# Attention and a routed feed-forward on one Trainium2 core: the order of the steps on every engine is written anew

## The reference

```python
x = x + layernorm(attention(layernorm(x)))
x = x + layernorm(ffn(layernorm(x)))
# attention: 16 heads of 8, rotary positions, causal
att = softmax(where(causal, q @ k.T / sqrt(8), -1e10));  y = att @ v @ Wp + bp
# ffn: 16 experts of width 176, the best 2 per token by softmax gate, and a shared part of width 352
y = sum over the 2 experts of weight * ((silu(x @ w1 + b1) * (x @ w3 + b3)) @ w2 + b2)
z = (silu(x @ sw1 + sb1) * (x @ sw3 + sb3)) @ sw2 + sb2;  result = y + z
```

## Time and profile before

| | before |
|---|---|
| median of 3 runs | 1276.95 us (1274.19 to 1278.73) |
| profiled execution, its own time | 1279.9 us |
| span of that execution | 1277.7 us |
| mean granted TensorE clock | 0.934 |
| TensorE busy | 1099.5 us, 86% |
| VectorE busy | 867.2 us, 68% |
| ScalarE busy | 703.4 us, 55% |
| GpSimd busy | 840.7 us, 66% |

### The profile page before, as it was taken

How to read it: one execution, slowest core, us unless ns; L and a number is a source line. 1 busy time by engine, 2 the same in 40 slices (tenths; PEclk the granted TensorE clock), 3 DMA queues, 4 the chain that set the end, 5 groups by cost and what they waited for, 6 DMA issues and landing times.

```text
span 1277.7 us, 26879 instructions
## 1 busy us (share of the span) xinstructions
PE 1099.5 (86%) x8520; PEld 711.3 (56%) x8520; DVE 867.2 (68%) x2283; ACT 703.4 (55%) x1569; POOL 840.7 (66%) x984
## 2 busy tenths in 40 slices
PE   1479989999999999999999999999866999999900
PEld 1344555655656565565656656566334788888700
DVE  4386778777787776777778777777222666666676
ACT  0115666565656656565665666666621555555534
POOL 4544558677777767777777776665664466666667
PEclk9768999999999999999999999999887999999955
DMA  4322223313143231323323133223312354454366
GB/s 88 120 80 88 80 62 118 99 54 103 56 122 98 77 101 54 101 69 124 96 65 103 55 104 108 71 75 81 107 44 81 89 157 124 120 156 123 97 212 187
DMA packets 104681, 126.16 MB, mean 99 GB/s; under 512 B 17422, under 2 KB 85344, under 8 KB 99936
## 3 DMA queue, kind: packets, MB, share of 16 engines
q1 hardware_dynamic: 91638, 104.54, 27.9%
q0 software_dynamic: 8704, 18.11, 4.0%
q10 hardware_dynamic: 4202, 1.81, 0.5%
HBM read 78.06 MB, written 45.42 MB: 97 GB/s over the span
## 4 chain that ended last, share of the span: by engine, by line
PE 72%; DVE 15%; issue 3%; DMA 2%; POOL 2%; ACT 1%; SPq 1%; POOLq 0%; DVEq 0%; ACTq 0%
PE heads_ps L1474 11%; PE wide L1502 10%; PE score L1464 10%; PE wide L1624 7%; PE wide L1439 4%; DVE mx L1276 4%; PE wide L1504 4%; PE score L1452 3%; PE wide L1605 3%; PE wide L1606 3%; PE score L1596 2%; PE wide L1535 2%; DVE chosen L1123 2%; PE wide L1622 2%; PE misc L1482 2%
## 5 line engine op out<-in xcount | busy, mean ns | idle before, releaser
L946 ACT ACTIVATE values<-score 128x512 f32<-128x512 f32 (+1 forms) x704 | 370.0, 556 | 199.9 <-PE score L1464 194.1
L1276 DVE TENSOR_REDUCE mx<-wide 128x2 f32<-128x1024 f32 (+3 forms) x384 | 387.6, 1040 | 85.5 <-PE wide L1504 84.8
L833 POOL TENSOR_SCALAR_AFFINE_SELECT values<-values 128x512 f32<-128x512 f32 x256 | 163.8, 643 | 169.0 <-ACT values L946 166.8
L1502 PE MATMUL wide<-qk 72*128 72x512 bf16 (+3 forms) x1024 | 248.8, 310 | 14.1 <-DVE mx L1276 6.0
L1464 PE MATMUL score<-qk 75*128 75x512 bf16 (+3 forms) x1024 | 237.3, 305 | 10.1 <-DMA qk<-mparts 6.2
L878 POOL DMA_INDIRECT token_scratch<-spread,e_id x144 | 137.9, 958 | 96.4 <-issue 74.5
L1504 PE MATMUL wide<-maskneg,identb 128*128 128x128 bf16 x1024 | 201.1, 225 | 0.0
L1474 PE MATMUL heads_ps<-values 128*32 128x512 f32 (+3 forms) x2048 | 176.1, 444 | 0.2 <-issue 0.2
L822 POOL DMA_INDIRECT sorted_scratch<-zr,places x128 | 129.9, 1015 | 56.4 <-DVE places L1217 19.1
L1464 PEld LDWEIGHTS score<-qk 75*128 75x128 bf16 x1024 | 88.0, 99 | 123.2 <-ACT values L946 51.7
L1502 PEld LDWEIGHTS wide<-qk 72*128 72x128 bf16 x1024 | 102.2, 100 | 90.8 <-DVE mx L1276 26.1
(11 more groups left out here) (196 smaller groups left out, 2003.2 us busy)
## 6 DMA issues: line engine op xcount, KB each, us to landing
qk<-parts_scratch SPq DMA_DIRECT2D x192, 192.0 KB
parts_scratch<-spread SPq DMA_DIRECT2D x16, 768.0 KB, 8.3
qk<-sorted_scratch SPq DMA_DIRECT2D x144, 66.0 KB
front<-token_scratch SPq DMA_DIRECT2D x16, 512.0 KB, 3.8
xt<-attn_x SPq DMA_DIRECT2D x16, 256.0 KB, 8.5
xr<-attn_x SPq DMA_DIRECT2D x16, 256.0 KB, 8.9
x_scratch<-z SPq DMA_DIRECT2D x16, 256.0 KB, 6.7
shared_scratch<-s_out SPq DMA_DIRECT2D x16, 256.0 KB
```

The source lines that it names most:

```text
L833: nc.gpsimd.affine_select(out=prob[n][:, :, 0:P], in_=prob[n][:, :, 0:P], compare_op=ALU.is_ge, fill=0.0, base=0, pattern=[[0, HG], [1, P] ...
L946: nc.scalar.activation(free_ap(prob[kb][:, hs_[0], :], [[1, N * len(hs_)]]), score[SCORE_RING.buffer(b, step)][:, 0:N * len(hs_)], ACT.Exp ...
L1276: nc.vector.tensor_reduce(mx[:, h0:h0 + len(hs_), j:j + 1], src, axis=AX.X, op=ALU.max).then_inc(p1_max, 1)
L1502: nc.tensor.matmul(o, q4[e][0:ROWS, h, j * P:(j + 1) * P], k4[e][0:ROWS, h, 0:L], start=True, stop=False)
```

## The change

The three strings are replaced. Every step that was there is still there, with the same instructions. Each engine's order, the order of the users of the ring buffers, and the offsets of some steps differ: among others `chosen`, G0, U0, H0, H1, d0, d1 and d2 go from offset -2 to -1 and stand late in the list; Q and `cos` stand with offset 3 instead of 4; R has offset 4, `zrstd`, Z and `residual` 0; `heads2` of a batch stands in the iteration after it; masks of groups 0 to 2 stand in the iteration before their batch. UPS, the table by which G finds the buffer of its U, is sorted by number, since U0 now stands behind U1 and U2 in the string.

```diff
--- before.py
+++ after.py
@@ -87,27 +87,27 @@
 
 
 ORDER = (
-    "s0.0 p19@0 s0.1 R p20@0 s0.2 v3.1@-1 v3.2@-1 v3.3@-1 s0.3 p21@0 s0.4 heads3@-1 p22@0 mask0.1 s0.5 s0.6 p23@0 "
-    "chosen@-2 H0 mask0.2 v0.0 s0.7 s0.8 d0 G0 Y U0 p0 s0.9 s0.10 K p1 place mask0.3 s1.0 W s1.1 d1 p2 mask1.0 "
-    "s1.2 p3 s1.3 zrstd zstats v0.1 p4 s1.4 s1.5 U1 s1.6 s1.7 V v0.2 M1@0 Z v0.3 mask1.1 N1@0 s1.8 G1 O1@0 stats residual "
-    "s1.9 p5 p6 heads0 s1.10 v1.0 v1.1 s2.0 rstd mask1.2 d2 mask1.3 p7 s2.1 mask2.0 s2.2 normal p8 rrstd rnormal "
-    "s2.3 p9 s2.4 mask2.1 s2.5 rstats T v1.2 mask2.2 v1.3 s2.6 p10 mask2.3 s2.7 second H1 v2.0 s2.8 third0 "
-    "mask3.0 p11 s2.9 heads1 p12 U2 s2.10 G2 p13 s3.0 rX s3.1 H2 d3 mask3.1 d4 v2.1 v2.2 mask3.2 s3.2 third1 "
-    "mask3.3 sin0@4 X@4 sin1@4 s3.3 rL s3.4 d5 v2.3 M0 choose N0 p14 Q@4 O0 s3.5 s3.6 v3.0 mask0.0@1 p15 s3.7 p16 s3.8 "
-    "rexp D s3.9 cos@4 sin2@4 p17 d6 p18 sin3@4 s3.10 heads2 d7 "
+    "s0.0 heads2@-1 s0.1 p18@0 rrstd Q rnormal s0.2 p19@0 mask2.1 s0.3 v3.1@-1 v3.2@-1 v3.3@-1 s0.4 p20@0 s0.5 "
+    "heads3@-1 s0.6 mask2.2 mask2.3 p21@0 s0.7 p22@0 s0.8 K H2 rstd normal mask3.0 s0.9 p23@0 place s0.10 cos Y "
+    "d3 s1.0 v0.0 M1@0 s1.1 N1@0 p0 W mask3.1 s1.2 O1@0 s1.3 v0.1 v0.2 v0.3 zstats d4 mask3.2 p1 s1.4 U1 G1 s1.5 "
+    "mask3.3 p2 v1.0 third0 d5 s1.6 p3 s1.7 p4 s1.8 s1.9 p5 d6 heads0 third1 s1.10 p6 s2.0 p7 s2.1 v1.1 mask0.0@1 "
+    "sin0@4 s2.2 p8 d7 mask0.1@1 s2.3 v1.2 v1.3 H0@-1 p9 s2.4 s2.5 rstats p10 s2.6 U2 G2 s2.7 heads1 sin1@4 s2.8 "
+    "p11 p12 s2.9 stats mask0.2@1 s2.10 T d0@-1 v2.0 M0 s3.0 s3.1 mask0.3@1 V N0 d1@-1 d2@-1 v2.1 mask1.0@1 s3.2 "
+    "rX O0 p13 s3.3 s3.4 zrstd@0 p14 v2.2 sin2@4 v2.3 Z@0 mask1.1@1 s3.5 p15 s3.6 second rL choose sin3@4 s3.7 "
+    "mask1.2@1 mask1.3@1 residual@0 p16 rexp R@4 s3.8 mask2.0@1 H1@-1 X@4 chosen v3.0 s3.9 G0@-1 U0@-1 s3.10 D "
+    "p17 "
 )
 START = (
-    "stats@1 rstd@1 X@1 normal@1 sin0@1 sin1@1 Q@1 sin2@1 cos@1 splits@1 fold@1 sin3@1 R@1 rstd@2 normal@2 "
-    "third0@1 third1@1 stats@2 sin0@2 sin1@2 sin2@2 T@1 sin3@2 R@2 rstd@3 normal@3 third0@2 second@1 X@2 V Q@2 "
-    "cos@2 third1@2 stats@3 sin0 T@2 X sin1 sin2 Q sin3 p0 R rstd p1 normal p2 p3 p4 cos p5 p6 second@2 p7 p8 p9 "
-    "p10 p11 stats p12 T sin0@4 sin1@4 p13 p14 X@4 M0 p15 N0 second O0 Q@4 p16 sin2@4 p17 cos@4 third0 third1 sin3@4 "
-    "mask0.0@1 p18 "
+    "rstd@1 stats@1 normal@1 sin0@1 X@1 sin1@1 sin2@1 sin3@1 R@1 Q@1 rstd@2 normal@2 V stats@2 third0@1 third1@1 "
+    "cos@1 splits@1 fold@1 T@1 second@1 sin0@2 sin1@2 X@2 Q@2 cos@2 stats@3 sin2@2 T@2 X sin3@2 R@2 rstd@3 "
+    "normal@3 third0@2 sin0 third1@2 Q sin1 p0 second@2 p1 p2 sin2 p3 p4 p5 rstd p6 p7 p8 sin3 stats normal p9 R "
+    "p10 p11 third0 p12 p13 mask0.0@1 M0 p14 third1 sin0@4 sin1@4 mask0.1@1 mask0.2@1 X@4 N0 cos sin2@4 mask0.3@1 "
+    "mask1.0@1 mask1.1@1 p15 mask1.2@1 O0 mask1.3@1 p16 sin3@4 p17 T R@4 second mask2.0@1 "
 )
 DRAIN = (
-    "v3.1@-1 v3.2@-1 v3.3@-1 chosen@-2 heads3@-1 K place Y d0 d1 W d2 zstats U0 G0 zrstd Z d3 U1 residual G1 H0 "
-    "rstats U2 rrstd rnormal rX rL G2 choose rexp H1 d4 d5 H2 d6 d7 chosen K@-1 counts@-1 place@-1 blocks@-1 "
-    "ends@-1 D d0@-1 d1@-1 d2@-1 d3@-1 d4@-1 d5@-1 d6@-1 d7@-1 U0@-1 rows@-1 U1@-1 U2@-1 G0@-1 G1@-1 H0@-1 G2@-1 "
-    "H1@-1 H2@-1 D@-1 "
+    "heads2@-1 rrstd rnormal v3.1@-1 v3.2@-1 v3.3@-1 heads3@-1 K H2 place Y d3 W zstats d4 U1 G1 d5 d6 d7 H0@-1 "
+    "rstats U2 G2 d0@-1 d1@-1 d2@-1 rX rL choose rexp H1@-1 chosen G0@-1 U0@-1 D K@-1 counts@-1 H2@-1 place@-1 "
+    "blocks@-1 ends@-1 rows@-1 d3@-1 d4@-1 U1@-1 G1@-1 d5@-1 d6@-1 d7@-1 U2@-1 G2@-1 D@-1 "
 )
 OFFSET = dict(stats=4, rstd=4, normal=4, X=3, Q=3, cos=3, sin=3, R=3, T=3, second=3, third=3, V=1, p=1, M=1, N=1, O=1, s=0, v=0,
               mask=0, heads=0, Y=-1, W=-1, zstats=-1, zrstd=-1, Z=-1, residual=-1, rstats=-1, rrstd=-1, rnormal=-1,
@@ -164,7 +164,7 @@
 
 
 GATE = next(s for s in STEPS if s.what == "rL")
-UPS = [s for s in STEPS if s.what == "U"]
+UPS = sorted((s for s in STEPS if s.what == "U"), key=lambda s: s.n)
 
 
 def program(nc, x, Wq, bq, Wk, bk, Wv, bv, Wp, bp, gate_w, gate_b, w1, b1, w3, b3, w2, b2,
```

## The result

| | before | after |
|---|---|---|
| median | 1277.28 us (1274.19 to 1278.73, 4 runs) | 1213.91 us (1213.65 to 1214.54, 4 runs) |
| ratio, 95% interval | | 0.9508 (0.949 to 0.9526) |
| span of the profiled execution | 1277.7 us | 1211.3 us |
| mean granted TensorE clock | 0.934 | 0.941 |

The forecast was 1239 us, with a range of 1220 to 1266. The change gained 66.4 us of span where 38.1 were forecast.

The account below looks back on a forecast made before the run. TensorE was taken to bound the iterations, so only idle time could be won: 21 + 0.6 + 2 - 1 + 7 + 5 + 3.5 = 38.1 us off 1279.9, forecast median 1239 us, range 1220 to 1266.

Parts of the forecast that it names:

- What bounds the kernel: Full iterations: TensorE bounds them, its 51.7 us busy stay, and a new order can give back only 2.4 of 54.1 us.
- K's wait: TensorE's idle time ahead of step K, waiting for VectorE's `chosen`, goes: 1.8 us gained per iteration.
- New waits: Full iterations: TensorE newly waits for VectorE's run from `zstats` to T or for masks, 0.3 us per iteration, ends 0 and 1.5.
- VectorE becomes the bound: Rival, iterations: T or a `p` comes 1.5 us late in each and the clock keeps dropping, 1259 us; chance 0.20.
- Iterations 3 to 11: Full iterations: each gains 2.4 - 0.3 = 2.1 us besides the clock, 21 us for iterations 3 to 12.
- The best case of the rivals: Rival, whole kernel: no new wait, no clock drop, fill and drain at their better ends, 1222 us; chance 0.07.
- The clock: TensorE's six half-clock stretches go with its waits of near 2 us: 7 us gained, ends 0 and 8.6.
- iteration 15: It gets U0 of batch 14 (1.9 us) and p18, in part into idle time: 1 us longer.
- Iterations 0 and 1: Waits of s2.0 for the maxima's DMA go, 4.3 us, against p18 and U0 moved in: net 2 us gained.
- The fill: Before iteration 0: Q of batch 3 and p18 leave, X and Q of batch 1 come earlier: 5 us gained, ends 2 and 8.
- The drain: After iteration 15: W(15) and SyncE's row blocks start earlier, against U0, D and late scatters: 3.5 us gained, ends 0 and 6.
- The slower case: Rival, iterations: GpSimd passes VectorE's lateness on through late masks, TensorE waits and its clock drops, 1292 us; chance 0.07.

Follow-up runs that it names:

- a_reduce_plus1: The changed kernel with one more VectorE reduction of p10 per iteration, 1.2 us, into a spare tile: 1232.35 us, ratio 0.9656 to the kernel before.
- a_v_split: The changed kernel with its blocks of 32-column `v` products split, six more per iteration: 1290.16 us on a slower chip, ratio 0.9728 to the kernel before.
- a_control: The changed kernel run again, unaltered, for comparison within its set: 1215.14 us, ratio 0.952 to the kernel before.
- a_v_merged: The changed kernel with the lone v1.1 and v2.1 put beside their neighbours, four passages less: 1218.81 us, ratio 0.9551 to the kernel before.
- b_chosen_early: The kernel before with `chosen` moved from behind p23 to behind p20: 1335.46 us on a slower chip, ratio 1.0078 to the kernel before.
- a_chosen_late: The changed kernel with `chosen` put back in front of p21, at offset -2: 1332.46 us on a slower chip, ratio 1.005 to the kernel before.
- a_reduce_plus2: The changed kernel with two more VectorE reductions of p10 per iteration, 2.4 us together: 1312.58 us on a slower chip, ratio 0.9993 to the kernel before.
- a_reduce_plus3: The changed kernel with three more VectorE reductions of p10 per iteration, 3.6 us together, into a spare tile: 1297.7 us, ratio 1.0164 to the kernel before.
- a_scatters_first: The changed kernel with the last batch's scatters d3 to d7 ahead of H1 and H2 in the drain: 1262.17 us, slower chip, ratio 0.9512 to the kernel before.
- a_maxima_mid: The changed kernel with M1, N1 and O1 started at s1.5, not behind v0.0: 1261.47 us on a slower chip, ratio 0.9583 to the kernel before.
- a_scatters_again: The changed kernel with scatters d3 to d7 ahead of H1 and H2 in the drain, a repeat: 1252.15 us, slower chip, ratio 0.9521 to the kernel before.

## Why the prediction missed, step by step

**What bounds the kernel: right as to the engine, wrong as to the floor.** "No step is added or dropped, so the 51.7 us of TensorE's work stay" is the step that failed, and with it "a new order can give back only its idle time: 2.4 us of 54.1". The 51.7 was busy time, and I took busy time for work. A matmul's end is modelled in the profile, so busy time also covers short gaps between the starts. The distances between the starts of steps, in an undisturbed iteration of either kernel (us, before and after):

```
s0.10 (K's wait behind it)  2.17  0.28      K itself    0.59  0.40
s1.9 (p5's wait)            0.75  0.22      s1.0 to W   0.57  0.31
s2.3                        0.41  0.31      p8          0.54  0.45
whole iteration            54.10 50.59
```

K was counted at 1.8 and gave 2.1 (1.90 + 0.19); p5 at 0.4 and gave 0.53; W at 0.2 and gave 0.26. These make 2.9, s2.3 and p8 0.2 more, and the last 0.45 is the sum of some thirty steps of ±0.02 to 0.14, mostly passages to and from `v` and M. a_reduce_plus1 shows the undercount by itself (0.59 shown, 1.0 paid), a_v_split the passages (1.3 us of them, unseen). The Trainium skill ("Perfetto Trace Analysis", "Identifying the Most-Contended Engine") warns that matmul busy share is no good measure of how near TensorE is to its limit, since pipelined instructions look smaller; the trace agrees that the share misleads: from 224 to 740 us a_control is busy for 516.0 us of 516.0 with iterations of 50.6 us, and a_v_merged for 514.3 with 50.9, without one wait in the list.

**New waits, 0.3 us per iteration.** The list shows none, and the distances between steps find under 0.1 us at any one place of the changed kernel: 0.3 x 10 was too much. But the reason I gave, 1.8 to 2.8 us left to VectorE in its run from `zstats` to T, was wrong: the run ends well only as a whole, and inside it each `p` has a deadline of its own, two buffers on. At p11 the margin is about 0.4 us (a_reduce_plus1), at p8 0.5 (a_v_merged). At three places there is none: in the changed kernel itself Y, U2 and p16 start 0.06 us behind the VectorE reduction that frees their buffer (medians of iterations 3 to 11), for instance p16:

```profile
366.67 0.96 DVE L1276 TENSOR_REDUCE mx<-wide 128x2 f32<-128x768 f32 x1 [0.24 <-PE wide L1504]
...
367.68 0.28 PE L1502 MATMUL wide<-qk 72*128 72x256 bf16 x1
```

The rival "VectorE becomes the bound" was wrong by its price (1259 us), but VectorE already touches TensorE at these places, for some 0.03 to 0.08 us each.

**Iterations 3 to 11.** 39.3 us: 7.9 of clock and 31.4 of the rest, 3.5 each, against 2.1. Of the 28.3 us by which the forecast missed the span, 12.5 lie here and 14.8 in iterations 0, 1 and 15; the rest nearly cancels. The best case of the rivals, 1222 us, was 8 us too long as well, for it kept the same floor.

**The clock.** Forecast 7, found 7.9 in iterations 3 to 11, and more in iterations 0, 12 and 15. For the full iterations the reasoning held: each half-clock stretch there followed a wait of TensorE of 1.7 to 2.9 us, in the kernel before, b_chosen_early, a_chosen_late, a_reduce_plus2 and a_reduce_plus3, and none followed one of 0.6 us. But two sentences of it were wrong. The clock was not full up to 252.9 us: it was half from 96 to 103 and from 120 to 123.5, in iteration 0. And the rows that spoke against a clock that small idle times make fall end at 911.6, just short of a stretch that stands behind small idle times alone. The rule of the Trainium skill ("TensorE: Matmul & The Clock Gate", "A second HAM failure mode: psum-queue depth-cycling") is that small gaps between groups of matmuls can make the clock swing. In iterations 2 to 14 of the changed kernel the trace shows nothing of it, with the clock at 1.00; in iteration 15 the kernel before, a_scatters_first and a_v_split agree with it.

**Iterations 0 and 1: forecast 2 us gained, found 9.6; iteration 15: forecast 1 us longer, found 6.2 shorter.** I costed the waits and not the half clock beside them, though the rows of before had it: clock 0.89 in iteration 0 and 0.93 in iteration 15. Kernel before, waits of TensorE from 92 to 140 us, then its clock at two places, and the waits ahead of the second:

```profile
PE wide L1502 <- DVE mx L1276: 2.5, 3, 1.5
PE score L1464 <- DMA qk<-mparts: 2.0, 1, 2.0
...
96.00:103.00 7.00, 6.95 (x36) 3.40 (x35) 4.08 (x5) 2.59 (x6) 4.01 (x5) 0.51 0.71 221
...
912.00:919.00 7.00, 6.98 (x22) 2.86 (x22) 0.55 (x2) 2.81 (x6) 4.30 (x6) 0.52 0.97 301
...
905.23 0.63 PE L1482 MATMUL misc<-ident,oT 128*128 128x128 f32 x4 [0.86 <-DVE mparts L1284]
...
908.19 0.60 PE L1464 MATMUL score<-qk 75*128 75x512 bf16 x2 [0.47 <-DMA qk<-mparts]
909.26 0.88 PE L1464 MATMUL score<-qk 75*128 75x512 bf16 x2 [0.47 <-ACT values L946]
910.35 0.34 PE L1464 MATMUL score<-qk 75*128 75x384 bf16 x1 [0.20 <-ACT values L946]
```

Seven microseconds at half clock are worth up to 3.5 us, and that twice, and 3.4 us more of it stood in iteration 0. For iteration 0 an estimate from the rows adds up: 3.8 us of waits gone (4.9 before, 1.1 after), some 4 us of clock, less 0.55 for p18, against 7.5 found. But no run put one of these back alone. For iteration 15 the clock is shown to be worth such a sum: one wait of 1.5 us put back brings half clock and costs 5.3 us (a_maxima_mid). That is not the wait of the kernel before, though, whose longest was 0.86 us. Which of its four small waits, or all together, brought the half clock there, no run shows.

**The fill: right**, 5 forecast, 4.8 found. Its parts weren't tested.

**The drain: forecast 3.5, found 0.2.** K(15) moved from 32.5 to 32.8 us behind the drain's start, with U0 and D in front of it, and the scatters behind H1 and H2 ended late; I had named both and priced them too low. a_scatters_again gives the price of the second, 2.1 to 2.5 us; the rest of the 3.3 missed is open.

**The slower case** fell outright: no wait of TensorE from 224 to 730 us is left, for a mask or anything else.

## What to carry to other kernels

When the bounding engine is TensorE, take its floor from the distances between the starts of steps where nothing waits, not from its busy time: each wait costs some 0.2 to 0.4 us more than its idle time, each passage between tile shapes about 0.1, and one wait of 1.5 us or more can cost as much again, or more, in half clock. Price a margin at each buffer's own deadline, against whichever engine frees that buffer, not over a whole run of work. And read a granted clock under 1.00 in any stretch, the short ones at the ends too, as time that may be won back with the waits before it, several small ones included.

## What the hardware showed that I had not expected

- The half clock can follow waits shorter than the stretch that it then lasts: 1.72 us idle, then a mean of 0.74 over 6 us; 1.5 us, then 0.71 over 15 us. A wait of that length doesn't always bring it (6 of 10 in the kernel before). The levels are 2.4 GHz (1.00) and 1.2 GHz (0.50).
- It can also come behind small waits alone: 0.86, 0.47, 0.47 and 0.20 us ahead of the stretch at 912 us in the kernel before, 0.45 and 0.20 us in a_scatters_first.
- A passage between 128-column score tiles and 32-column `v` products costs 0.09 to 0.14 us each way and is shown as busy; one between bf16 and f32 over the same 128 columns costs nothing that these distances show (0.17 us for the score step either way).
- A `p` that has to wait starts 0.06 us behind the end of the read that frees its buffer, and a wait so short that the tail of the last matmul covers it is in no list.
- VectorE's L1123, two operands in SBUF, took 2.37 us beside GpSimd's R and 0.29 us away from it. The Trainium skill ("SBUF — State Buffer", "Who interferes with whom") has such a pair contend for one read port; the trace agrees.
